# Five products that nobody reads, added to every batch of a two-layer decoder kernel: three ahead of r1.z, one ahead of rf.h, one ahead of n.proj

## The reference

```
x = _layernorm(x + _L0_attn_ref(x, ...))       # Nystrom attention: 16 heads of 8, 64 landmarks, 6 Newton steps
x = _layernorm(x + _L0_xattn_ref(x, ctx, ...))  # attention to ctx, 16 heads of 8, distance bias
x = _layernorm(x + _L0_ffn_ref(x, ...))         # 8 experts, the best one is taken
x = _layernorm(x + _L1_attn_ref(x, ...))        # causal attention, 16 heads of 8
x = _layernorm(x + _L1_xattn_ref(x, ctx, ctx, mask, ...))  # attention to ctx, 16 heads of 64, masked
x = _layernorm(x + _L1_ffn_ref(x, ...))         # gelu(x W1) W2, W1 and W2 mixed from 32 low-rank factors
```

## Time and profile before

| | |
|---|---|
| median of 3 runs | 2502.62 us (2498.36 to 2503.68) |
| the profiled execution: its own time | 2506.76 us |
| its span, first to last instruction | 2504.8 us |
| busy: PE, DVE, ACT, POOL | 91%, 78%, 58%, 15% of the span |
| mean granted TensorE clock | 0.968 |

### The profile page before, as it was taken

How to read it: one execution, slowest core, us unless ns; L and a number is a source line. 1 busy time by engine, 2 the same in 40 slices (tenths; PEclk the granted TensorE clock), 3 DMA queues, 4 the chain that set the end, 5 groups by cost and what they waited for, 6 DMA issues and landing times.

```text
span 2504.8 us, 95982 instructions
## 1 busy us (share of the span) xinstructions
PE 2274.5 (91%) x40798; PEld 1852.9 (74%) x40798; DVE 1957.2 (78%) x6166; ACT 1450.2 (58%) x5093; POOL 387.7 (15%) x530
## 2 busy tenths in 40 slices
PE   7899999999999999999999999999999999999896
PEld 4777777777777777777777777777777777777763
DVE  3568788888878888888888888888888788888753
ACT  3346566566656665656656565665665565656531
POOL 2111111111111111111111111111111111111111
PEclk9899999999999999999999999999999999999997
DMA  4200000000000000000000000000000000000000
GB/s 195 89 7 9 5 7 9 9 9 9 9 4 8 9 9 9 9 4 8 8 9 9 9 9 5 7 9 9 9 9 9 4 8 9 9 9 8 3 6 3
DMA packets 29962, 35.79 MB, mean 14 GB/s; under 512 B 3544, under 2 KB 28128, under 8 KB 28384
## 3 DMA queue, kind: packets, MB, share of 16 engines
q1 hardware_dynamic: 29536, 29.65, 3.4%
HBM read 27.54 MB, written 2.10 MB: 12 GB/s over the span
## 4 chain that ended last, share of the span: by engine, by line
PE 53%; DVE 28%; ACT 14%; issue 4%; POOL 0%; DMA 0%; SPq 0%; POOLq 0%; ACTq 0%; DVEq 0%
PE ps L501 29%; PE ps L504 8%; ACT probs L1101 4%; PE ps L768 4%; DVE probsT L1388 3%; PE ps L852 3%; ACT probs L1086 2%; PE ps L900 2%; PE ps L785 2%; ACT ey L1024 2%; DVE x_rows L1250 2%; DVE small L1291 2%; DVE probs L1520 1%; PE ps L689 1%; DVE qk_v L1376 1%
## 5 line engine op out<-in xcount | busy, mean ns | idle before, releaser
L1141 POOL TENSOR_TENSOR small<-small,weights 128x1 f32<-128x1 f32 x256 | 149.2, 583 | 1139.6 <-DVE small L1239 1139.6
L1049 ACT ACTIVATE probs<-ps,small 128x128 f32<-128x128 f32 x1024 | 286.1, 384 | 28.8 <-DVE small L1381 27.3
L1388 DVE COPY probsT<-ps 128x512 f32<-128x512 f32 x384 | 263.1, 685 | 35.1 <-PE ps L504 31.6
L504 PE MATMUL ps<-weights,probs 128*128 128x128 f32 x1536 | 253.0, 289 | 26.1 <-ACT probs L1049 14.7
L1381 DVE TENSOR_REDUCE small<-ps 128x4 f32<-128x512 f32 x384 | 254.2, 683 | 16.9 <-PE ps L852 8.9
L1152 POOL TENSOR_TENSOR probs<-probs,small 128x256 f32<-128x256 f32 x128 | 108.7, 849 | 875.5 <-DVE small L1517 875.5
L504 PEld LDWEIGHTS ps<-weights,probs 128*128 128x128 f32 x1536 | 177.7, 145 | 79.4 <-ACT probs L1049 41.0
L968 ACT COPY x_T<-ps 128x128 f32<-128x128 f32 x128 | 34.1, 267 | 302.4 <-PE ps L504 302.4
L1101 ACT ACTIVATE probs<-ps,small 128x128 f32<-128x128 f32 x512 | 181.6, 375 | 15.3 <-DVE small L1381 13.8
L501 PE MATMUL ps<-wz,ss 64*64 64x72 f32 x6144 | 154.5, 226 | 31.4 <-DVE wz L1333 31.3
L1332 DVE SCALAR_TENSOR_TENSOR wz<-ey,ss 128x256 f32<-128x256 f32 x320 | 142.4, 445 | 49.3 <-ACT ss L1009 36.5
(11 more groups left out here) (203 smaller groups left out, 5438.5 us busy)
## 6 DMA issues: line engine op xcount, KB each, us to landing
weights<-in_wpack SPq DMA_DIRECT2D x3, 1759.0 KB
fc_A<-in_b SPq DMA_DIRECT2D x2, 2048.0 KB, 14.4
fc_A<-in_a SPq DMA_DIRECT2D x2, 2048.0 KB, 12.1
x_in_T<-in_xT SPq DMA_DIRECT2D x32, 64.0 KB, 1.8
x_in_rows<-in_x SPq DMA_DIRECT2D x32, 64.0 KB, 1.8
ctx_T<-in_ctxT SPq DMA_DIRECT2D x32, 64.0 KB, 1.9
ctx_rows<-in_ctx SPq DMA_DIRECT2D x32, 64.0 KB, 1.9
mask_i<-in_mask SPq DMA_DIRECT2D x32, 64.0 KB, 1.9
```

Of the source, the lines that this page charges most:

```text
L504: return nc.tensor.transpose(dst, src, ident)
L1049: ins = nc.scalar.activation(probs(s, g)[:, j], bank(s, SCORE_BANK[g], 128 * j, 128), ACT.Exp, bias=sm(s, "nb", 4 * g + j, 1), scale=-1.0)
L1141: nc.gpsimd.tensor_tensor(sm(s, out), sm(s, ve), w("mhalf"), ALU.pow).then_inc(sem(done, s), 1)
L1388: V.tensor_copy(probsT(s, n % 4).rearrange("p a b -> p (a b)"), bank(s, 2)).then_inc(sem("pT", s), 1)
```

## The change

`keep_clock` gets a third source of products that nobody reads, and this one holds in all batches. Ahead of each `r1.z` it issues three, ahead of each `rf.h` one, ahead of each `n.proj` but the first one. Each is `one(bank(..., 256, 128), ident, w("n_q"))`: a float32 product of 128 by 128 by 128 of two tiles that lie in SBUF all the time, into columns 256 to 383 of a bank of the same stream (bank 2 of the lane, bank 1 of Nystrom). It waits for nothing and signals nothing. That makes 3 x 32 + 32 + 31 = 159 products, 318 MATMUL records and as many weight loads. Nothing else changes; DVE, ACT, POOL and SP have the same instructions in the same order.

```
+KEEP_REST = {"r1.z": 3, "rf.h": 1}
+KEEP_NYSTROM = {"n.proj": 1}
...
                 reached.add((lane, number))
+                if lane == NYS:
+                    for _ in range(KEEP_NYSTROM.get(name, 0) if number else 0):
+                        one(bank(NYS, 1, 256, 128), ident, w("n_q"))
+                else:
+                    for _ in range(KEEP_REST.get(name, 0)):
+                        one(bank(lane, 2, 256, 128), ident, w("n_q"))
```

## The result

| | changed | before, same chip |
|---|---|---|
| median of 6 runs each | 2515.63 us (2507.37 to 2522.45) | 2501.51 us (2497.61 to 2503.68) |
| ratio, 95% interval | 1.0046 (1.0034 to 1.0059) | |
| profiled execution: own time, span, clock | 2507.37, 2505.4, 0.976 | 2506.76, 2504.8, 0.968 |

The forecast was 2488.8, range 2478 to 2499. The change made the kernel slower by 0.46% (the medians lie 14.1 us apart). The sign was wrong, not only the size. (The profiled execution is the fastest of the six of the changed kernel. The clocks of the other five are 0.967 to 0.974, so they had more dips than the one that we can look at.)

What follows compares the result with a forecast made beforehand. PE sets the pace in most of the run, so its clock dips slow the kernel. Products cost 0; removing A and B gains 30 x (73.78 - 73.32) = 13.8 us, from 2502.62 to 2488.8, range 2478 to 2499.

Steps and rivals of the forecast that it cites:

- What a dip costs: Mean batch lengths of 73.32 and 74.93 us in two stretches give 1.38 us per clock dip, 72.63 per batch without one.
- A: Clock dip right after `r1.z`, where PE sat idle 0.85 us for DVE's z; expected to go with 0.67 us of products.
- B: Clock dip at `rf.h`, after gaps ahead of `n.proj` and `rf.h`, 0.91 us; expected to go with 0.44 us of products.
- C: Clock dip after 8-column products `n.W5` and `n.w`; expected to stay in every other batch; C-only stretch: 894.2 to 1334.1 us.
- Price of a product at its place: One product takes 0.22 us of PE's queue; those ahead of `r1.z`, `n.proj` and `rf.h` fit existing waits, cost 0.
- Rival 1: The products are free but do not hold the clock: no gain, no cost, 2502.6 us; chance 0.10.
- The doubt about turns: Trainium skill says transposes do not bring full clock; places around A and B may be emptier, leaving the time at 2502.6.
- The change part by part: Prices the five products per batch at `r1.z`, `n.proj` and `rf.h`: between 0 and 1.11 us per batch, taken as 0.
- D dips: Not in the forecast: clock dips found in the changed kernel a little after `n.y0`, in a row of very small products.
- rival 4: C becomes rarer: one dip in three batches gives 2468 with none, 2482 at that rate; chance 0.12 for fewer than two in five.
- rival 3: C takes the place of A and B, in every batch: 6.9 us more than before, 2509.5 us; chance 0.03.
- rival 2: The products do not fit the gaps and are paid, up to 1.11 us per batch: 2523; decides from 0.46; chance 0.04.

Runs made afterwards that it cites:

- e3: Kernel before plus three products at `r1.z`, one at `n.proj`, bf16, 512 columns; `n.b` products merged, so 2561 instructions per batch as before: 2492.49 us, 0.9907.
- e4: e3 with its four added products 8 columns wide instead of 512, so the same instructions without the streaming: 2508.56 us, 0.9981 of the kernel before.
- e5: e3 with the product at `n.proj` 8 columns wide, the three at `r1.z` full: 2500.38 us, 0.996 of the kernel before.
- e6: e3 with two products 8 wide at `r1.z` and an added one 512 wide at `rf.h`: 2495.64 us, 0.9939 of the kernel before.
- e1: The changed kernel with the same five products 8 columns wide instead of 128: 2524.45 us, 1.0051 of the kernel before.
- e2: Kernel before with 62 tiny bf16 products (124 instructions) in batch 1 only, shifting all later batches against the block borders: 2570.84 us, 1.0235.
- e8: e3 with one product at `rf.h` as well, so all three places of the change, 2563 instructions per batch: 2499.21 us, 0.9959 of the kernel before.
- e11: e3 run again on another chip, the same as a repeat of the changed kernel: 2491.66 us, 0.9923 of the kernel before.

## Why the prediction was wrong

**What bounds the kernel: right. What a dip costs: a little too high.** A, B and C are the dips. Where A and B were removed and nothing else happened (e3) the batches take 73.16 us against the 73.32 read from the C-only stretch. A dip costs about 1.2 us there, not 1.38. The stretch from 1999.6 to 2224.4, from which 1.38 was worked out, also has the kernel's one wait for `ctx_T`, which the prediction counted as dip:

```profile
2166.24 1.13 PE L501 MATMUL ps<-x_firstT,weights 128*128 128x128 f32 x8 [1.06 <-issue]
```

The forecast's 13.8 us did not rest on this price, but on the mean lengths of batches.

**Price of a product at its place: right.** Distances of 1.19, 0.83 and 0.69 us; z wait 6.2 us for 7.7.

**Do the products hold the clock: right.** No A or B dip in the middle, and the same kernel with narrow products has them all (e3 against e4, 16 us; e5, e6 by place). Rival 1 is out. The doubt about turns in "What the products give" did not matter.

**The step that failed** is the balance in "The change part by part": "It removes nothing, moves nothing", "No wait and no signal is added, and no other engine's queue is touched", and from it "the cost lies between 0 and 1.11 us per batch. I take 0". It counted the time that the products take on PE and looked for waits only between engines. It left out that every product is also four instructions in PE's own stream, which is fetched in blocks of 256. The order on PE moved nothing, but each later instruction moved against the blocks' borders, by 20 per batch. The kernel before stood at a favourable place: 2561 is ten blocks and one, and its borders cut the dense run of small products in two from batch 2 on. In place of the 0 there came 10.0 us of stalls in 12 batches, and eight D dips. No row of before named this; one could have led there, 323 instruction packets for 82721 instructions of PE. The single issue wait of 1.1 us could not: it is the wait for `ctx_T`.

The sum for the profiled execution, 2507.37 us against the 2493.0 forecast for it, 14.4 us too low:

- stalls at a border: +10.0 us;
- waits for `ctx_T`: 2.2 us for the 1.1 of the kernel before, +1.1 us;
- eight D dips, 8 x 1.2 = +9.6 us;
- C dips: 10 in the 30 batches from the second `n.ln` on, where one in every other batch would be 15: 5 x 1.2 = -6.0 us. That is the direction of rival 4; rival 3 is out.

That is +14.7 us for 14.4. The batches agree with it:

```profile
L508 PE MATMUL ps<-weights,x_first x31: 327/328/332, 160.0 to 2374.4; 128*128 128x128 f32 x31
```

(2374.4 - 160.0) / 30 = 73.81 us per batch, 0.49 more than the forecast's 73.32, which over 30 batches is 14.8 us. The cost of stalls and D dips, 19.6 / 31 = 0.63 us per batch, is above the 0.46 at which rival 2 decides. Rival 2's price was possible and its mechanism wrong: nothing was paid beside the products. For the median, 8 us above the profiled execution, seven more dips would do (8 / 1.2), and the lower clocks of the other executions, 0.967 to 0.974 for 0.976, point to that; which kind they are no trace shows.

**What stays open.** (1) Why PE resumes only 1.2 to 1.6 us after the packet has landed. The block fetched after one border is needed at the next, so no more than one block was ready ahead; how PE holds its blocks the traces do not show. (2) Without alignment the products gave far less than the 16 us they give with it: the ratios of e1 (1.0051) and of the changed kernel (1.0046, 1.0028) differ by 0.2% at most, and their intervals overlap. A stalled batch has its dip at D, and perhaps would have had one at A or B otherwise; this wasn't tested. (3) C was not cured. (4) The waits for `ctx_T` go with the fetch as well: in the thirteen traces, from 250 us on, 14 loads of `ctx_T` ran beside an instruction packet and took 2.6 to 3.4 us, the other 364 at most 2.1 us. That the packet holds up the load was not tested.

## What to carry to other kernels

Before adding or removing PE instructions in an unrolled loop, count the instructions per turn of the loop and see where the borders of the 256-instruction blocks fall, above all whether a whole block comes to lie in a run of very small products; compare PE's issue waits before and after, and look whether a load landed just ahead of one before it is put down to the fetch. If a small edit moves the time with no wait to show for it, run two controls: the same number of instructions without the work (e4), and the old kernel with a single shift (e2). Judge an edit only with the block's border held in place: the same places filled with products were 0.3 to 0.5% slower without it and 0.4% faster with it (e8), and with one product less 0.8 to 0.9% faster (e11, e3).

## What the runs showed of the hardware

- Instruction fetch can hold up PE in straight-line code: 36.1 us in 30 waits (e2), up to 1.6 us each, though the queue takes only 0.8% of the 16 engines' span.
- From one border to the next PE needed at least 3.0 us in these 30 batches: it had used the 256 instructions up after 2.13 to 2.16 us, the packet began 0.7 to 1.1 us after the border, and PE went on 1.2 to 1.6 us after it had landed.
- It did so in a run of short instructions: `r1.v1` has 32 products, each with its weight load, in 0.44 us, 64 instructions at 7 ns each. A batch has ten borders, and with that run cut in two by one (e3) no issue wait stands at any of them.
- A gap of 0.8 to 1.6 us in front of light work was followed by a dip to 0.50 each time in e2 (30 dips for 30 waits), so a stall is paid nearly twice: 62 us for 36.1 us of waiting.
- Four products of 512 columns per batch that nobody reads, put in waits that exist anyway, kept the clock up and were worth 16 us of 2509.
